# A warping path found from both ends: 64 steps on 128 lanes in place of 104 steps on 64 lanes

## The reference

```
x1  = x + (causal attention of layernorm(x), squared scores, 16 heads of 16) @ Wo
s   = layernorm(x1)                                  # "student", 1024 rows
D   = sqrt(max(|c|^2 + |s|^2 - 2 c.s, 0))            # 77 x 1024, c = context rows
R[i,j] = D[i,j] + min(R[i-1,j], R[i,j-1], R[i-1,j-1])
path   = from R's last corner back to the first, each step to the least of the three
x2[j]  = x1[j] + sum of c[i] over the path's cells (i, j)
out    = x2 + mlp(layernorm(x2))                     # 256 -> 1024 -> 256, gelu
```

## Time and profile before

| | before |
|---|---|
| median of 3 runs | 953.76 us |
| the profiled execution, its own time | 952.99 us |
| its span in the profile | 951.2 us |
| PE busy | 785.1 us (83%) |
| DVE busy | 557.7 us (59%), 2527 instructions |
| ACT busy | 441.6 us (46%) |
| POOL busy | 143.1 us (15%) |
| chain that ended last | PE 48%, DVE 39%, ACT 5%, issue 5%, DMA 2% |
| mean granted clock of TensorE | 0.91 of full |

### The profile page before, as it was taken

The page is one execution under the profiler, slowest core; times in us unless marked ns, Lnnn a source line. Parts: engine busy times, 40 slices in busy tenths (PEclk is TensorE's granted clock), DMA queues, the critical chain, the costliest instruction groups (busy, mean ns, idle before and its releaser), DMA issues.

```text
span 951.2 us, 12631 instructions
## 1 busy us (share of the span) xinstructions
PE 785.1 (83%) x3919; PEld 383.6 (40%) x3919; DVE 557.7 (59%) x2527; ACT 441.6 (46%) x664; POOL 143.1 (15%) x310
## 2 busy tenths in 40 slices
PE   4879977898999888999779598638799934599998
PEld 3443322244333342322333133324485623357657
DVE  6645564415461229999989983359969888521001
ACT  2257786766677556767548476103302200133120
POOL 2113123112211202312112121001001000100100
PEclk9999988999999998999899798667899967599999
DMA  4663333013232202223302211010000001100001
GB/s 140 197 211 89 123 101 111 12 56 111 60 147 74 73 12 77 58 93 106 100 18 70 73 30 23 7 21 6 9 28 27 11 23 43 32 1 12 33 1 45
DMA packets 52222, 58.58 MB, mean 62 GB/s; under 512 B 22719, under 2 KB 31907, under 8 KB 52155
## 3 DMA queue, kind: packets, MB, share of 16 engines
q1 hardware_dynamic: 51067, 53.57, 19.1%
q0 software_dynamic: 1088, 4.19, 1.4%
HBM read 36.24 MB, written 21.50 MB: 61 GB/s over the span
## 4 chain that ended last, share of the span: by engine, by line
PE 48%; DVE 39%; ACT 5%; issue 5%; DMA 2%; SPq 0%; DVEq 0%; ACTq 0%
PE psO L1114 9%; PE psS L1097 8%; DVE FOLD L876 7%; PE psW L1268 7%; PE psS L1258 6%; DVE FOLD L897 5%; PE psW L1162 4%; DVE FOLD L874 3%; PE psW L1185 3%; DVE FOLD L895 3%; PE psW L1153 3%; PE psW L1169 2%; ACT ARENA L734 2%; DVE FOLD L873 2%; DVE STATS L943 2%
## 5 line engine op out<-in xcount | busy, mean ns | idle before, releaser
L734 ACT ACTIVATE ARENA<-psS 128x1024 f32<-128x1024 f32 (+3 forms) x384 | 301.2, 811 | 117.1 <-PE psS L1097 114.1
L1097 PE MATMUL psS<-ARENA 96*128 96x512 bf16 (+3 forms) x768 | 195.6, 346 | 30.5 <-ACT ARENA L734 29.4
L1114 PE MATMUL psO<-ARENA 128*32 128x512 f32 (+3 forms) x1536 | 175.3, 530 | 7.3 <-DVE ARENA L831 4.7
L667 POOL TENSOR_SCALAR_AFFINE_SELECT ARENA<-ARENA 128x256 f32<-128x256 f32 x256 | 110.2, 434 | 430.5 <-ACT ARENA L734 429.1
L1097 PEld LDWEIGHTS psS<-ARENA 96*128 96x128 bf16 x768 | 57.4, 100 | 221.1 <-ACT ARENA L734 126.1
L1268 PE MATMUL psW<-W2E,ARENA 128*128 128x256 f32 x512 | 114.7, 386 | 16.8 <-DVE ARENA L1077 16.1
L1268 PEld LDWEIGHTS psW<-W2E,ARENA 128*128 128x128 f32 x512 | 98.7, 193 | 33.0 <-DVE ARENA L1077 16.5
L798 ACT ACTIVATE ARENA<-psS,BEFF 128x512 f32<-128x512 f32 x64 | 43.6, 687 | 123.0 <-PE psS L1258 123.0
L1153 PE MATMUL psW<-IDENT,XX 128*128 128x128 f32 x192 | 36.2, 343 | 49.0 <-DVE XX L964 49.0
L876 DVE TENSOR_TENSOR_SCAN FOLD<-FOLD,MORE 64x37 f32<-64x37 f32 x208 | 69.8, 336 | 7.3
L1162 PE MATMUL psW<-XX,ARENA 128*128 128x512 f32 x128 | 63.8, 601 | 8.1 <-DVE ARENA L979 6.8
(11 more groups left out here) (116 smaller groups left out, 827.4 us busy)
## 6 DMA issues: line engine op xcount, KB each, us to landing
ARENA<-qk_parts SPq DMA_DIRECT2D x192, 128.0 KB, 2.7
qk_parts<-ARENA SPq DMA_DIRECT2D x16, 768.0 KB, 3.5
out<-ARENA SPq DMA_DIRECT2D x16, 256.0 KB, 2.1
X<-in_x POOLq DMA_DIRECT2D x3, 1024.0 KB, 7.5
dist<-ARENA SPq DMA_DIRECT2D x4, 425.0 KB, 3.7
MORE<-dist SPq DMA_DIRECT2D x32, 52.6 KB
path<-MORE SPq DMA_DIRECT2D x52, 32.4 KB
X<-in_x SPq DMA_DIRECT2D x1, 1024.0 KB, 5.6
```

The costliest lines, as they stand in the source:

```text
L667: pool.affine_select(out=blk, in_=blk, compare_op=ALU.is_ge, fill=0.0, base=0, pattern=[[0, 2], [1, P]], channel_multiplier=-1).then_inc(s ...
L734: nc.scalar.activation(A[:, (2 * G + a) % A_PAIRS, :, 0:N], psS[:, a, :, 0:N], ACT.Square).then_inc(s_sq, 1)
L1097: ins = nc.tensor.matmul(psS[:, a, j, 0:N], KST[0:STACK, g % 2, 2 * a + j, kt * P:(kt + 1) * P], QST[0:STACK, g % 2, 2 * a + j, q0:q0 + N] ...
L1114: ins = nc.tensor.matmul(psO[32 * j:32 * j + 32, o % 2, q0 - qc * HALF:q0 - qc * HALF + N], V1[:, kt, GH * g + j], A[:, (2 * G + j // 2) % ...
```

## The change

The matrix is cut between rows 38 and 39. Rows 0 to 38 are run from the first corner on lanes 0 to 63; rows 76 down to 39, with the columns reversed, from the last corner on lanes 64 to 127, in the same instructions. A block is now 40 columns, 26 blocks, and `T` = 39 + 25 = 64 steps in each direction. A new unit `meet` finds the column where the two halves join at the least total, and the walk back starts there in both. The context rows get the same order (39 rows, a gap, 38 reversed rows: 102 partitions) in a new unit `order`, which also makes the norms. The distances come 8 steps at a time. A second copy of each group of marks, with columns and blocks reversed (`TURNED`), is made for the lower half. Warp 1 no longer has steps ahead of `quick_ready(0, 0)`; all of it is woven behind. The core of the diff:

```diff
-W_BLK = 28
-CB = -(-L // W_BLK)
-T = S + W_BLK - 1
+UPPER, LOWER = 39, 38
+W_BLK, CB, EDGE = 26, 40, 8
+T = UPPER + W_BLK - 1
+FINAL = UPPER - 2
+SPAN = 64 + LOWER
-CH, GRP, RING = 13, 8, 16
-PAIR, LANES = 2, 64
+CH, GRP, RING, HOLD = 8, 8, 16, 32
+PAIR, WAYS, LANES = 2, 2, 128
...
-    warp = lambda w: ([("warp_start", w)] + [("forward", w, t) for t in range(T)] + [("moves", w)]
+    warp = lambda w: ([("warp_start", w)] + [("forward", w, t) for t in range(T)] + [("moves", w), ("meet", w)]
...
-    for b, fill, due in ((0, up + [("context", i) for i in range(B)] + front(1) + mixes + down, {}),
+    for b, fill, due in ((0, up + [("context", i) for i in range(B)] + [("order", i) for i in range(B)] + front(1) + mixes + down, {}),
...
-    plan += half_back(3, 1) + second[:1 + HALF // CB] + quick_ready(0, 0)
+    plan += half_back(3, 1) + quick_ready(0, 0)
...
-    plan += flat(woven(pieces, second[1 + HALF // CB:], [4 if piece[0][0] == "out" else 1 for piece in pieces])) + quick_ready(2, 1)
+    plan += flat(woven(pieces, second, [4 if piece[0][0] == "out" else 1 for piece in pieces])) + quick_ready(2, 1)
...
             def dist_out(b, h):
                 sp.wait_ge(s_dn, b * 2 + h + 1)
+                sp.wait_ge(s_edge, b // PAIR + 1)
...
+                for way in range(WAYS):
+                    blocks = slice(0, MID) if h == way else slice(MID, W_BLK)
+                    sp.dma_start(by_row(dist_dram, b, way)[:, blocks],
+                                 BACK[b][3][rows_of(way)].rearrange("p (w c) -> p w c", c=CB)[:, blocks]).then_inc(s_dist_out[b][h], 16)
...
+                for lanes, marks in ((slice(0, 64), MARK), (slice(64, 128), TURNED)):
+                    sp.dma_start(by_lane(path_dram, w)[lanes, g * GRP:(g + 1) * GRP], marks[lanes, n % 2]).then_inc(s_path_out[w][n % 2], 16)
...
+                for way, marks in enumerate((by_row(path_dram, b, 0), by_row_mirrored(path_dram, b))):
+                    blocks = slice(0, MID) if late != way else slice(MID, W_BLK)
+                    sp.dma_start(PT[rows_of(way), b % PAIR].rearrange("p (w c) -> p w c", c=CB)[:, blocks], marks[:, blocks]
+                                 ).then_inc(s_pt_in[b][late], 16)
...
+                    for i in range(PAIR):
+                        for h in range(2):
+                            sp.wait_ge(s_dist_out[PAIR * w + i][h], 16 * WAYS)
...
-                    nc.scalar.activation(DN[0:S, h * HALF:(h + 1) * HALF], DSQ[0:S, h * HALF:(h + 1) * HALF],
+                    nc.scalar.activation(DN[rows_of(0), EDGE + h * HALF:EDGE + (h + 1) * HALF], DSQ[rows_of(0)], ACT.Sqrt)
+                    nc.scalar.activation(DN[rows_of(1), EDGE + (1 - h) * HALF:EDGE + (2 - h) * HALF][:, ::-1], DSQ[rows_of(1)],
                                          ACT.Sqrt).then_inc(s_dn, 1)
...
+            def meet(w):
+                tail = KIND[:, FINAL:T]
+                vec(nc.vector.tensor_tensor(out=tail, in0=tail, in1=KEEP[:].unsqueeze(2).to_broadcast([LANES, T - FINAL, CB]), op=ALU.mult))
+                ends = ROWS[:, FINAL % HOLD + 1:FINAL % HOLD + 1 + T - FINAL]
+                vec(nc.vector.tensor_tensor(out=ends, in0=ends, in1=LASTROW[:].unsqueeze(2).to_broadcast([LANES, T - FINAL, CB + 1]),
+                                            op=ALU.mult))
+                settled()
+                vec(nc.vector.tensor_reduce(ENDROW, ends.rearrange("p t c -> p c t"), axis=AX.X, op=ALU.add))
+                settled()
+                for way in range(WAYS):
+                    mine, others = slice(64 * way, 64 * way + 64), slice(64 - 64 * way, 128 - 64 * way)
+                    vec(nc.vector.stream_shuffle(OTHER[mine], ENDROW[others, 1:CB + 1], MIRROR))
+                vec(nc.vector.tensor_tensor(out=CROSS, in0=ENDROW[:, 1:CB + 1], in1=ENDROW[:, 0:CB], op=ALU.min))
+                settled()
+                vec(nc.vector.tensor_tensor(out=TOTAL, in0=CROSS, in1=OTHER[:, ::-1], op=ALU.add))
+                settled()
+                def of_all(x, values, op):
+                    best = BEST[:, x:x + 1]
+                    vec(nc.vector.tensor_reduce(best, values, axis=AX.X, op=op))
+                    settled()
+                    vec(nc.vector.tensor_copy(LANE, best.to_broadcast([LANES, 32])))
+                    settled()
+                    vec(nc.vector.transpose(ALLOF, LANE))
+                    settled()
+                    vec(nc.vector.tensor_reduce(ONE[:, x:x + 1], ALLOF, axis=AX.X, op=op))
+                    settled()
+                    return ONE[:, x:x + 1]
...
-                nc.vector.tensor_tensor(out=MARK[:, n % 2], in0=UPTO, in1=REACH[:, r:r + GRP, 1:CB + 1], op=ALU.subtract).then_inc(s_path, 1)
+                nc.vector.tensor_tensor(out=MARK[:, n % 2], in0=UPTO, in1=REACH[:, r:r + GRP, 1:CB + 1], op=ALU.subtract).then_inc(s_mark, 1)
+                dve.wait_ge(s_mark, done + 1)
+                nc.vector.stream_shuffle(TURNED[64:128, n % 2], MARK[64:128, n % 2][:, :, ::-1], MIRROR).then_inc(s_path, 1)
...
+                elif kind == "order":
+                    _, b = u
+                    nc.vector.tensor_scalar(CTX[:, b], got[0:SPAN, 0:D], -0.5, None, ALU.mult).then_inc(freed, 1)
+                    dve.wait_ge(freed, made(*u))
+                    sq = R1[0:SPAN, 0:D]
+                    vec(nc.vector.tensor_tensor(out=sq, in0=CTX[:, b], in1=CTX[:, b], op=ALU.mult))
+                    settled()
+                    vec(nc.vector.tensor_reduce(AA[:, b:b + 1], sq, axis=AX.X, op=ALU.add))
+                    settled()
...
                 elif kind == "along":
-                    pe.wait_ge(s_pt_in[b][1], 32)
-                    if i < 2:
-                        pe.wait_ge(s_pt_in[b][0], 16)
+                    for late in range(2):
+                        pe.wait_ge(s_pt_in[b][late], 16 * WAYS)
```

More of the change, by code:

```diff
@@ L109 @@
 HALVED = ("qk", "value", "wo", "dist")
-SIZE = dict(qk=17, value=17, wo=17, dist=34, turn_x=5, turn_s=5, turn_f=5, up=5, w1=5, down=9, chain=5, coef=9, context=2, w_exp=5,
+SIZE = dict(qk=17, value=17, wo=17, dist=34, turn_x=5, turn_s=5, turn_f=5, up=5, w1=5, down=9, chain=5, coef=9, context=2, order=2, w_exp=5,
             mix=9, bias=4, stats=3, variance=2, root=1, rstd=1, normal=3, pause=4)
@@ L215 @@
 ON_SCALAR = ("turn_x", "qk", "value", "turn_s", "turn_f", "dist")
-ITEM_KINDS = ("context", "w_exp", "turn_x", "qk", "value", "wo", "turn_s", "dist", "coef", "chain", "up", "w1", "down", "along", "turn_f", "out")
+ITEM_KINDS = ("context", "order", "w_exp", "turn_x", "qk", "value", "wo", "turn_s", "dist", "coef", "chain", "up", "w1", "down", "along", "turn_f", "out")
 def layer(nc, x, ctx_in, Wq, Wk, Wv, Wo, W_exp, b_exp, up_w, up_b, down_w, W_con, b_con, down_b, out):
@@ L418, in layer @@
         s_reach = sem("s_reach")
[L419 removed]
+        s_path_out = [[sem(f"s_path_out{w}_{i}") for i in range(2)] for w in range(B // PAIR)]
         s_pt_in = [[sem(f"s_pt_in{b}_{h}") for h in range(2)] for b in range(B)]
@@ L641, in _, with lane_tables, step @@
                                      [64, 64 >> st, 2, 1 << st])).then_inc(s_widen, 1)
+            def lane_tables():
+                n = T - FINAL
+                count = [0]
+                def step(ins):
+                    ins.then_inc(s_lanes, 1)
+                    count[0] += 1
+                    pool.wait_ge(s_lanes, count[0])
+                step(pool.memset(LASTROW[:], 0.0))
+                step(pool.memset(KEEP[:], 1.0))
+                for q in range(PAIR * WAYS):
+                    lanes, way = slice(32 * q, 32 * q + 32), q // PAIR
+                    step(pool.affine_select(out=LASTROW[lanes], in_=LASTROW[lanes], compare_op=ALU.not_equal, fill=1.0,
+                                            base=1 - way, pattern=[[-1, n]], channel_multiplier=1))
+                    step(pool.affine_select(out=KEEP[lanes], in_=KEEP[lanes], compare_op=ALU.is_ge, fill=0.0,
+                                            base=1 - way, pattern=[[-1, n]], channel_multiplier=1))
+                    step(pool.iota(PLACE[lanes], [[2 * way - 1, CB + 1]], 1 if way else 2 * L, CB if way else -CB,
+                                   allow_small_or_imprecise_dtypes=True))
+                    step(pool.affine_select(out=LASTROW[lanes, 0:1], in_=LASTROW[lanes, 0:1], compare_op=ALU.is_ge, fill=1.0,
+                                            base=W_BLK - 1, pattern=[[0, 1]], channel_multiplier=-1))
             def x_in(b):
@@ L673, in _ @@
                     mask(*u[1:])
+                elif kind == "turn_s" and u[1] % PAIR == 0 and u[2] == 0:
+                    b = u[1]
+                    pool.wait_ge(s_parts_out, 64 * max(b + 2, 3))
+                    if b:
+                        for h in range(2):
+                            pool.wait_ge(s_dist_out[b - 1][h], 16 * WAYS)
+                    pool.memset(BACK[b][3][0:SPAN, 0:EDGE], BIG)
```

(9 more changed lines are left out.)

200 lines of the change are left out of this document (98 added, 102 removed).

## The result

| | before | after |
|---|---|---|
| median | 953.21 us (4 runs, 952.52 to 955.08) | 914.59 us (4 runs, 911.96 to 919.23) |
| the profiled execution, its span | 952.99, 951.2 us | 919.23, 917.5 us |
| DVE busy | 557.7 us | 489.3 us |
| mean granted clock | 0.91 | 0.93 |

The ratio is 0.9597, with a 95% interval of 0.9555 to 0.9639: 4% faster, as forecast in kind and inside the range, but 11.6 us above the 903 of the prediction.

A forecast was written before the change was run, and what follows sets the result against it. The warping path on DVE was taken to decide in three stretches, PE in the rest. The terms +1.5 - 18 - 39.3 + 4.7 = -51.1 against the 951.2 us span gave 900.1, forecast as 903 us, range 884 to 925.

The forecast's parts named there:

- the end: After warp 1's last marks: all `along` products wait for them and two more transfers are issued, +4.7 us.
- One warp, 104 us: DVE work of each warp: 104 us in place of 148, 44 less, with `meet` at 7.2.
- the rival that ended slower: Warp steps: 128 lanes at half rate, 1.2 us a step, about 1045 us in all; chance 0.03.
- Warp 1, -39.3: Behind the attention: sums start earlier and the warp is shorter, last marks at 774.5 in place of 813.85.
- Small costs before: Start and early attention: `order` units +0.5 (-3 to +5), square root in two instructions +1 (0 to 4), POOL 0.
- The strips: Transfers of 38 rows use two DMA engines: 3 us more at each warp's start, 3 at the end, 909; chance 0.1.
- Batches 2 and 3, -18: Warp 0 in the attention: first stretch -5, second -13, together -18 us (0 to -40).
- The wait for distances: Warp 0's start: both halves of a matrix must be in DRAM before the first chunk is read, +2 (0 to 4).
- The +2 for `meet` as one block: Warp 0's first stretch: 7 us in which DVE empties no PSUM bank, two banks cover about half, +2.
- PE becomes the bound there: Warp 0's stretches: DVE, relieved of some 20 and 23 us, could finish in 102 and 80, so PE decides.
- the sign: Batches 2 and 3: PE busy above 90% would show the forecast.
- Neither rival: Attention: gives nothing back, 921 us, chance 0.15; or DVE was all of the bound, 882 us, chance 0.12.

The follow-up runs named there:

- again: The changed kernel unaltered, measured and profiled once more; 914.75 us, ratio 0.9578 to the kernel before.
- order_later: The changed kernel with the four `order` units moved from batch 0's attention into batch 1's; 908.61 us, ratio 0.9519.
- join_parts: The changed kernel with `meet` cut into four units that the planner spreads; 914.65 us, ratio 0.9579.
- pad_warp1: The changed kernel with a dead 128x40 DVE copy in every forward step of warp 1; 921.05 us, ratio 0.9644.
- the move alone: The kernel before with only warp 1's 13 forward steps moved behind the first sums of batch 0; 947.92 us, ratio 0.9935.
- split38: The changed kernel with transfers of 38 rows cut into 32 and 6 rows, in both directions; 907.2 us, ratio 0.951.
- front_loaded: split38 with more steps of warp 1 between its first units (other weights in the list behind the attention); 901.32 us, ratio 0.9446.
- mended: split38 and order_later together; 902.03 us, ratio 0.9462.
- both: split38, order_later and the weights of front_loaded together; 899.2 us, ratio 0.9419.
- pad_warp0: The changed kernel with a dead 128x40 DVE copy in every forward step of warp 0; 922.54 us, ratio 0.9676.
- no_join: The changed kernel keeping only the mask product of `meet`, without the join search; walks back start in the middle column; 902.89 us, ratio 0.947.

## Why the prediction was right, and where it missed

Its sum was -51.1. With means over the traces that share a stage, the terms came out so:

| term | predicted | measured | from |
|---|---|---|---|
| start | 0 | +2.4 | 57.2 over twelve traces with the change, 54.8 over the two without |
| batches 0 and 1 | +1.5 | +6.7 | 281.8 over nine traces, 275.1 |
| batches 2 and 3 | -18 | -16.4 | 255.3 over after, again, order_later, join_parts, pad_warp1; 271.7 |
| behind the attention, to the last scan | -39.3 | -39.5 | 172.7, 212.2 |
| the end | +4.7 | +8.1 | 26.1, 18.0 |

The sum is -38.7, 12.4 short of the forecast; the medians say 11.6.

- **One warp, 104 us.** Nearly right in its parts where alone: backward scans at the end of warp 1 take 0.30 and stand 0.63 apart (0.615 predicted), forward ones 0.65 (0.63), the turned copy takes 0.51 (0.5), and 128 lanes with 40 columns take 0.63 a step where 64 lanes with 37 took 0.60, so the rival that ended slower falls. `meet` was put at 7.2; its instructions sum to 8.0 (4.87 for the three large ones, 3.1 for 15 small), because the strided reduction takes 2.18 in place of 1.31. The range for it (6 to 12) holds that. DVE's busy time fell by 68, not 80: the prediction took the pitch of the steps for busy time, and the gaps between dependent instructions don't count as busy. A window of five backward steps of the kernel after has DVE busy for 2.79 of 3.14 us:
```profile
767.41:770.55 3.14, 0.00 (x0) 0.00 (x0) 2.79 (x20) 0.00 (x0) 0.00 (x0) 0.50 0.23 42
```
  With such a tenth, 160 fewer steps of 0.61 us have 11 us less of gaps, by estimate; that is nearly all of the difference.
- **Warp 1, -39.3.** Right to 0.2 us, which is luck, since its two parts were each nearly 4 off: the first `hidden` came 17.3 us sooner after batch 3 (predicted 13.5, and 13.9 by the move alone), and from there the last scan took 140.7, where the forecast had some 137 (774.5 less 636, and less the last group of marks).
- **Small costs before: the failed step.** I priced four `order` units at +0.5 (-3 to +5) because "PE can pass only two of them ahead". With them in batch 0 the two batches measured +6.7, with them in batch 1 +1.5, which is the whole term as I had it. I had counted DVE's 5.7 us and asked who else needs DVE. The 4 us or so up to the 25th product came by PE's order instead, where scores stand behind transpositions that wait for DVE, and ACT behind the scores. The norms that went had held up the same place nearly as long, which is why the batch has lost nothing yet at that point. What I had no term for is the stretch up to the 137th product, 3.4 us longer by the means and at a lower clock; how much of it is the clock and how much the shifted list stays open.
- **The strips: a rival that was true.** I argued that the share of 0.91 meant nearly all engines. The Trainium skill, page "DMA: Bandwidth & Descriptors", section "Why a DMA increments its semaphore by 16 and not by 1", gives the largest number up to 16 that divides the slowest dimension of both sides, which is 2 engines for 38 rows and 11 for 77. The measured shares, 0.17 and 0.91, have the ratio 0.19, the rates 30 and 154 GB/s too, and 2 to 11 is 0.18: by that rule, the traces agree, and my reading of the share was wrong. It had cost me 3.4 of the end (22.6 with the strip cut is what I had forecast, 18.0 + 4.7) and as much at warp 0's start, 7.5 together. The rival's own price, 3 + 3, was a good one.
- **Batches 2 and 3, -18.** Near by offsets. Split, the forecast was -5 and -13 by stretch of warp 0, the batches gave -8 and -9. The wait for distances was put at +2 (0 to 4); the first step came 5 to 7 us later after batch 1 than before (28.8), 3.2 in split38 with the strip cut. With that cut the two batches take 249.4 (mean of split38, front_loaded, mended and both), 22 less than before. The +2 for `meet` as one block was nothing (join_parts). And "PE becomes the bound there" was wrong: the busy share I had named as the sign (over 90%) came in the forward stretch (94%), yet pad_warp0 and no_join show DVE's work still costing there, while in the backward stretch the share is 84% and the sign failed outright. Neither rival holds either: the attention gave 16 to 22 us, not 0, and not the 39 of DVE as all of the bound. In the forward part (first scan to first backward scan) it gave 13 to 16 of the 20 us of relief (98.1 and 95.2 in place of 111.0), in the backward scans 18 of 23 (88.0 in place of 105.9); the later first step took 6 to 7 of this back, and from the last backward scan to the end of batch 3 it is 34.4 us in place of 26.0. DVE so ends its warp ahead of PE now. That DVE decides in the forward part and PE behind it is my reading; only the first has runs for it.
- **The start** is no effect that I can show: instructions that the change doesn't touch ran slower in the first 45 us of the first trace after (one group of 20 matmuls took 11.14 us in place of 9.35; from 35 to 40 us the granted clock was 0.50), and with the change the first scores come anywhere from 54.7 to 59.3 (before: 53.5 and 56.0). The 2.4 is within that spread.

## What to carry to other kernels

Halving a serial chain of small instructions gave back on the path most of what stood alone, 33 of 44 us where the other engines waited for it (39.5 less the 6 of the move), and 16 of some 43, or 22 with the strips cut, where PE was itself 81 to 88% busy. When a partition range is cut for a new layout, look at the row counts of its transfers as well; 38 rows in place of 77 cost 7.5 us, and 32 + 6 cured it. And a short unit is priced by what stands behind it in every in-order engine that it touches, not by its own engine's time alone; and the busy time of an inserted instruction by what it adds to the pitch of its chain, here 0.09 us for copies of 0.22.
